# A graph kernel on one core: four accumulator banks for the adjacency products instead of two, and the small products of the edge lots moved into the gate banks

## The chip, the cores and the metric

The kernel runs on one core of one Trainium2 chip. The metric is the device time of one execution in microseconds (us), lower is better. The core has five instruction streams that the profile shows apart: TensorE (PE for its matmuls, PEld for its weight loads, PEq for its sequencer), VectorE (DVE), ScalarE (ACT), GpSimd (POOL) and SyncE (SP, which issues DMAs here). They run side by side and wait for each other through semaphores.

## The reference, cut to what matters

A graph with 6250 nodes of 48 features and 200,000 edges that are sorted by their destination. Five propagation steps with the normalised adjacency, a layer norm, a gated convolution over the edges, and a second layer norm:

```
def _L0_gnn_ref(x, edge_index):
    row = concat(src, loops); col = concat(dst, loops)
    deg = segment_sum(1, col); dinv = rsqrt(deg); w = dinv[row] * dinv[col]
    for _ in range(5):
        h = (1.0 - ALPHA) * segment_sum(w[:, None] * h[row], col) + ALPHA * x
    return h
def _L1_gnn_ref(h, edge_index, edge_attr, distances, atom_z, node_mult, ...):
    gate = _silu(edge_attr @ W1.T + b1) @ W2.T + b2 + adapt_logit
    cw = where(distances < CUTOFF, 0.5 * (cos(pi * distances / CUTOFF) + 1.0), 0.0)
    msg = gate * h[dst] * (cw * mj)[:, None]
    agg = segment_sum(msg, src) / clip(segment_sum(mj, src), 1e-08)
    return layernorm(h + agg) * gamma + beta
x = _layernorm(x + _L0_gnn_ref(x, edge_index))
x = _layernorm(x + _L1_gnn_ref(x, ...))
```

## The kernel before

The kernel builds the adjacency as a dense table of counts, multiplies with it five times, and does the gated convolution after that. Its stages follow each other in time. By the profiled execution: `index_edges` fills the first 160 us or so (it sorts out the edges and writes tables of keys); `adjacency` runs from about 160 to 1448 us; the propagation, which streams the adjacency from memory five times, begins at about 1475 us and goes over into the convolution, which ends at 4288 us.

**The adjacency.** The nodes form `NB` = 49 blocks of 128 (50 with padding). For each block `D` there are 64 groups of 128 edges (`GB` = 64, padded). A *turn* handles `PT` = 8 of these groups, so a block has `NBAT` = 8 turns. In each turn DVE writes two one-hot tiles, `ohb` (128 x 1024, L992) and `ohk` (128 x 784, L994), into one of `OB` = 8 slots; PE multiplies them in `batch` as two groups of four matmuls (L1031), and each group of four fills one accumulator bank of `pA`; ACT copies the bank of each group into the block's row `adj` (L1067, 128 x 392) and, when a block is complete, stores it (L1072, 1568 KB). The group `n` writes bank `n % 2` and first waits, on the semaphore `a_ev`, until ACT has copied group `n - 2` out of that bank. ACT waits on `a_grp` for the group. At the start of each turn PE increments `a_turn`, its *turn mark*.

**The edge lots.** The values of the gates do not depend on the propagation, so they are computed beside other work, in lots of 4096 edges (`NWIN` = 49 lots). 24 lots run inside the adjacency, interleaved with the turns by a list written out in the program; 25 run inside the propagation. The first loop of the adjacency (`DOUBLE` = 1 pass) does four blocks in 32 turns with one lot, the second loop has 23 passes of two blocks in 16 turns with one lot each. A lot has `MC` = 4 chunks of 8 steps (`CT` = 8), and takes this way through the engines:

- DVE's `fields`, `counts` and `ranks` find for each edge the slot in which its row will lie. They need two small products from PE: `labels` (L764, a 128 x 128 product, issued behind turn 0) and `offsets` (L769, 128 x 49, behind turn 4). Both go to the bank `w_pR`. ACT copies the offsets to `w_offb` (L774).
- For each chunk PE transposes the attributes (`transposes`, L731), ACT copies them (L799), PE computes the hidden layer (`hidden`, L740), ACT applies silu (L792, to `w_hid`), and PE computes the gates (`gates`, L749), 8 x 48 = 384 columns of bank `q % 2` of `w_pG`. In the second loop `pe_parts` issues these behind the odd turns: at turn 5 the gates of chunk 0, at 7 those of chunk 1, at 9 chunk 2, at 11 chunk 3.
- DVE's `rows_out` (L894 to L896, in turns 11 to 14) takes the gates into the rows `w_pay`. It waits for the gates and for `w_free`, which POOL gives when its scatter of an earlier chunk has landed.
- POOL scatters the rows to the table of slots: 32 indirect DMAs for each lot (L705), each issued by one instruction. Ahead of step `t` POOL waits for a turn mark of PE (`in_single`), so that the scatters are spread over the turns, two to a turn, a fixed number of turns behind:

```
pool.wait_ge(s_turn, w * MARKS + (DOUBLE * MARKS + 10 + t * MARKS // WT))
```

So the scatter of a lot runs from PE's turn 9 of its own pass to about turn 9 of the next. The order on each engine is the order in which the program is written; nothing reorders it.

## Time and profile before

| what | value |
|---|---|
| time of the kernel before, median of 3 runs | 4324.79 us (4321.98 to 4325.89) |
| time of the profiled execution | 4289.53 us |
| its span, first to last instruction | 4287.8 us |
| mean granted TensorE clock | 0.746 of full speed |
| busy: PE, DVE, POOL, ACT | 2739.1, 2747.3, 2377.7, 1372.9 us |

The time of an execution is what is measured; the span is read from the profile of one execution. That execution is 35.3 us shorter than the median, so durations of the profile are set against 4289.53 and only the difference is carried to the median. No engine is busy for more than 64% of the span, and the stages differ: in the adjacency another thing ends the waits than in the propagation. So the sum of an engine over the span says little here, and the adjacency has to be read by itself. In the rows below, a "releaser" is what ended the idle time of an engine. "issue" is time in which the engine waited for nothing that the profile shows; "remote" is a release that the profile could not put down to an instruction that ended just then.

### The profile page before, as it was taken

What the parts mean: (1) busy time and instruction counts of PE and PEld (TensorE: products, weight loads), DVE (VectorE), ACT (ScalarE), POOL (GpSimd) and SP (SyncE); (2) the same over time, 40 slices, a digit from 0 to 9 for tenths busy, and PEclk for the clock granted to TensorE, in tenths of its full rate; (3) what the DMA queues carried; (4) which work ended last, traced back from release to release, by engine and by line L of the source; (5) the groups of instructions that cost most, each with busy time, mean ns of one, the idle gap of its engine ahead of it and who ended that gap; (6) DMA issues with size and microseconds to landing.
All of it is one profiled execution on the core that took longest, in us unless ns stands there. A gap on an engine that the chain in (4) does not pass through costs nothing. (4 is left out here: it accounts for less than half of the span.)

```text
span 4287.8 us, 105568 instructions
## 1 busy us (share of the span) xinstructions
PE 2739.1 (64%) x35364; PEld 2335.0 (54%) x35364; DVE 2747.3 (64%) x5976; ACT 1372.9 (32%) x4059; POOL 2377.7 (55%) x2008
## 2 busy tenths in 40 slices
PE   0465555555565377787777787777366666666663
PEld 0343344433443366676676676667366666666662
DVE  3877677777776445554455445545787777777777
ACT  0443333333333111111011111111355555555552
POOL 1267777777777355565565555555344444444442
PEclk9955555555555589898998888888688777777776
DMA  4443333333522488787788787786455555555553
GB/s 182 184 157 137 136 137 136 147 141 136 149 89 89 180 287 298 258 309 286 284 296 297 265 295 285 276 284 239 152 203 186 203 187 199 182 203 180 202 183 92
DMA packets 228040, 871.37 MB, mean 203 GB/s; under 512 B 89155, under 2 KB 148419, under 8 KB 182786
## 3 DMA queue, kind: packets, MB, share of 16 engines
q1 hardware_dynamic: 166914, 728.89, 47.8%
q10 hardware_dynamic: 9696, 96.89, 5.7%
q0 software_dynamic: 51232, 42.56, 3.3%
q8 instruction: 171, 2.80, 0.3%
q14 instruction: 27, 0.22, 0.0%
HBM read 670.80 MB, written 197.52 MB: 203 GB/s over the span
## 5 line engine op out<-in xcount | busy, mean ns | idle before, releaser
L705 POOL DMA_INDIRECT slot_table<-w_pay,w_slot x1568 | 1786.5, 1139 | 1117.6 <-PEq L1217 506.6
L1219 PE MATMUL pL<-p_parts,p_adj 128*128 128x144 bf16 x12250 | 976.3, 241 | 360.0 <-issue 254.2
L1219 PEld LDWEIGHTS pL<-p_parts,p_adj 128*128 128x128 bf16 x12250 | 883.4, 105 | 446.2 <-issue 440.7
L1031 PE MATMUL pA<-ohk,ohb 128*128 128x98 bf16 x3200 | 359.7, 274 | 516.7 <-ACT adj L1067 267.6
L1031 PEld LDWEIGHTS pA<-ohk,ohb 128*128 128x128 bf16 x3200 | 256.8, 131 | 649.2 <-ACT adj L1067 339.0
L1587 ACT ACTIVATE h_all<-c_rows,c_ac 128x48 f32<-128x48 f32 x2401 | 561.0, 323 | 70.4 <-DVE c_ac L1558 70.4
L1463 POOL TENSOR_TENSOR c_msg<-c_msg 128x637 f32<-128x637 f32 x196 | 232.7, 1187 | 617.9 <-DVE c_msg L1525 617.9
L1067 ACT ACTIVATE adj<-pA 128x392 bf16<-128x392 f32 x800 | 369.6, 494 | 525.3 <-remote 260.7
L792 ACT ACTIVATE w_hid<-w_pH,b1c 96x512 f32<-96x512 f32 x196 | 133.7, 682 | 909.5 <-PE w_pH L740 444.2
L1662 PE MATMUL cG<-c_tabp,c_ohT 128*128 128x81 bf16 x7056 | 376.2, 224 | 3.2 <-issue 1.6
L1662 PEld LDWEIGHTS cG<-c_tabp,c_ohT 128*128 128x128 bf16 x7056 | 353.2, 114 | 4.5 <-DVE c_msg L1525 2.2
L1270 DVE TENSOR_REDUCE p_acc<-pL 128x144 f32<-128x432 f32 x100 | 53.2, 532 | 446.8 <-PE pL L1219 220.4
L1465 POOL TENSOR_TENSOR c_msg<-c_msg 128x637 f32<-128x637 f32 x196 | 324.6, 1656 | 15.4
L992 DVE TENSOR_TENSOR ohb<-io_k,pair_b 128x1024 bf16<-128x1024 bf16 x400 | 275.2, 688 | 66.9 <-DVE w_pay L896 14.2
L749 PE MATMUL w_pG<-w2T,w_hid 97*128 97x96 f32 x1568 | 292.8, 347 | 7.0 <-issue 7.0
L740 PE MATMUL w_pH<-w_attrT,w1T 80*96 80x512 f32 x392 | 288.8, 829 | 0.0
L1653 PE MATMUL cE<-c_cur,c_ohT 128*128 128x32 bf16 x7203 | 217.6, 181 | 110.1 <-ACT h_all L1603 70.3
L1637 PE MATMUL cO<-c_msg,c_ohs 128*128 128x147 bf16 x2401 | 244.5, 262 | 55.6 <-POOL c_msg L1465 54.3
L1498 DVE TENSOR_SCALAR c_ohT<-c_lanes,c_idx 128x3328 bf16<-128x3328 bf16 x196 | 271.9, 1387 | 6.8 <-DMA c_lanes<-lane_table 6.8
L1653 PEld LDWEIGHTS cE<-c_cur,c_ohT 128*128 128x128 bf16 x7203 | 209.2, 99 | 122.9 <-issue 122.8
L749 PEld LDWEIGHTS w_pG<-w2T,w_hid 97*128 97x128 f32 x1568 | 266.9, 256 | 8.4 <-issue 8.4
L1514 DVE TENSOR_TENSOR c_ohs<-c_iob,c_sl 128x1664 bf16<-128x1664 bf16 x196 | 241.7, 1233 | 0.0
(277 smaller groups left out, 3308.4 us busy)
## 6 DMA issues: line engine op xcount, KB each, us to landing
p_adj<-adj_table SPq DMA_DIRECT2D x250, 1568.0 KB
c_lanes<-lane_table SPq DMA_DIRECT2D x150, 768.0 KB, 6.5
adj_table<-adj ACTq DMA_DIRECT2D x50, 1568.0 KB
c_rows<-slot_table SPq DMA_DIRECT2D x255, 255.0 KB, 4.0
slot_table<-zero SPq DMA_DIRECT2D x42, 1249.5 KB
c_lanes<-lane_table SPq DMA_DIRECT2D x50, 832.0 KB
w_attr<-in_edge_attr_dram SPq DMA_DIRECT2D x49, 640.0 KB
slot_table<-w_pay,w_slot POOLq DMA_INDIRECT x1568
```

Of the source, the lines that this page charges most:

```text
L705: pool.indirect_dma_start(slotT, bass.IndirectOffsetOnAxis(ap=slot[:, t:t + 1], axis=0), pay[:, t, :], None, bounds_check=SLOTS - 1, oob_i ...
L740: nc.tensor.matmul(pH[0:2 * H, 0:n * P], w1T2[:, :], attrT[:, 0:n, :].rearrange("r t e -> r (t e)")).then_inc(s_h, 1)
L749: x_ = nc.tensor.matmul(pG[:, q % 2, i * 2 * H:(i + 1) * 2 * H], hid[:, i, :], w2T2[:, :])
L992: nc.vector.tensor_tensor(ohb[:, b % OB, :, :].rearrange("p q (a t) -> p q a t", t=2), twos(P), pair_b[:, at, :].unsqueeze(2).to_broadcast ...
L1031: m = nc.tensor.matmul(pA[:, n % 2, j * KG:(j + 1) * KG], ohb[:, b % OB, g * (PT // 2) + j, :], ohk[:, b % OB, g * (PT // 2) + j, :])
L1067: nc.scalar.activation(adj[:, u, :, n * PT:(n + 1) * PT].rearrange("p s (j d) -> p s j d", d=GR), pA[:, n % 2, 0:PT // 2 * KG].rearrange(" ...
L1219: x_ = nc.tensor.matmul(pL[:, half, o * H3:(o + 1) * H3], adj[:, q, n * P:(n + 1) * P], parts[:, n, :, :].rearrange("p t f -> p (t f)"), s ...
L1465: nc.gpsimd.tensor_tensor(part(c_, 2), part(c_, 1), upper[:, c_, 1, 0:n, :], ALU.subtract).then_inc(s_r2, 1)
L1498: nc.vector.tensor_scalar(ohT[:, k % 2, 0:2 * n, :].rearrange("p m e -> p (m e)"), lanes[:, c_, 0:2 * n * P], idx[:, :], None, ALU.is_equa ...
L1587: x_ = nc.scalar.activation(gx[:, k % 2, j, 0:H], rows[:, u, CUT[c_] + j, 0:H], ACT.Identity, bias=ac[:, k % 2, j:j + 1])
L1653: m = nc.tensor.matmul(pE[:, j * G:(j + 1) * G], ohT[:, k % 2, j, :], cur[:, u, t, :], start=t == 0, stop=t == 2)
L1662: m = nc.tensor.matmul(g_at(k, j), ohT[:, k % 2, n + j, :], tabp[:, CUT[c_] + j, t, :], start=t == 0, stop=t == 2)
```

## The change

The accumulator `pA` gets four banks in place of two: group `n` writes bank `n % 4` and waits until ACT has copied group `n - 4`. To have the banks, `w_pR` is given up. The labels now go to the free columns 384 to 511 of gate bank 1, the offsets to the columns 384 to 432 of gate bank 0. So that the gates of chunk 0, which write bank 0, do not meet ACT's copy of the offsets, these gates wait in addition for `w_offb` (in the adjacency; not in the propagation, where the order differs). `index_edges`, which runs earlier and had borrowed `w_pR`, gets a bank of its own for that time.

```diff
--- before.py
+++ after.py
@@ -378,7 +378,8 @@
                 pair = ew
                 bad_row = ps("bad_row", [1, 512], c=c)
                 pP = ps("pP", [P, 2, 1024], BF16, c)
-                pC, pZ, pQ = win.pR, win.pG, win.pT
+                pC = ps("pC", [P, 512], c=c)
+                pZ, pQ = win.pG, win.pT
                 s_dst, s_src, s_ew, s_et = s_edges
                 s_io = sem("i_io")
                 s_lo, s_lof, s_cnt, s_pre, s_sum = sem("i_lo"), sem("i_lof"), sem("i_cnt"), sem("i_pre"), sem("i_sum")
@@ -659,7 +660,10 @@
             pT = ps("w_pT", [P, 512], c=c)
             pH = ps("w_pH", [P, 512], c=c)
             pG = ps("w_pG", [P, 2, 512], c=c)
-            pR = ps("w_pR", [P, 512], c=c)
+            GATES = CT // 2 * 2 * H
+            assert GATES + P <= 512 and GATES + NB <= 512
+            offs = pG[:, 0, GATES:GATES + NB]
+            labs = pG[:, 1, GATES:GATES + P]
             seed = dram("seed", [CT * P, 4])
             s_init, s_kf, s_win, s_attr = sem("w_init"), sem("w_kf"), sem("w_win"), sem("w_attr")
             s_T, s_aT, s_h, s_hid, s_g = sem("w_T"), sem("w_aT"), sem("w_h"), sem("w_hid"), sem("w_g")
@@ -740,19 +744,21 @@
                 nc.tensor.matmul(pH[0:2 * H, 0:n * P], w1T2[:, :],
                                  attrT[:, 0:n, :].rearrange("r t e -> r (t e)")).then_inc(s_h, 1)
 
-            def gates(pe, w, q):
+            def gates(pe, w, q, offsets_first):
                 pe.wait_ge(s_hid, w * MC + q + 2)
 
                 pe.wait_ge(s_pay, w * MC + q + 1)
                 pe.sem_inc(s_pe, 1)
+                if q == 0 and offsets_first:
+                    pe.wait_ge(s_offb, w + 1)
                 for i in range(pairs_of(q)):
                     x_ = nc.tensor.matmul(pG[:, q % 2, i * 2 * H:(i + 1) * 2 * H], hid[:, i, :], w2T2[:, :])
                 x_.then_inc(s_g, 1)
 
-            def pe_parts(pe, w, n):
+            def pe_parts(pe, w, n, offsets_first=True):
 
                 if 2 <= n < MC + 2:
-                    gates(pe, w, n - 2)
+                    gates(pe, w, n - 2, offsets_first)
                 if 1 <= n < MC + 1:
                     hidden(pe, w, n - 1)
                 if n < MC:
@@ -761,17 +767,17 @@
             def labels(pe, w):
 
                 pe.wait_ge(s_diag, w + 1)
-                nc.tensor.matmul(pR[:, P:2 * P], ones_w[:, :], diag[:, :]).then_inc(s_lab, 1)
+                nc.tensor.matmul(labs, ones_w[:, :], diag[:, :]).then_inc(s_lab, 1)
 
             def offsets(pe, w):
 
                 pe.wait_ge(s_tot, w + 1)
-                nc.tensor.matmul(pR[:, 0:NB], before[:, :], tot[:, :]).then_inc(s_off, 1)
+                nc.tensor.matmul(offs, before[:, :], tot[:, :]).then_inc(s_off, 1)
 
             def act_offsets(act, w):
 
                 act.wait_ge(s_off, w + 1)
-                nc.scalar.activation(off_b[:, :], pR[:, 0:NB], ACT.Copy).then_inc(s_offb, 1)
+                nc.scalar.activation(off_b[:, :], offs, ACT.Copy).then_inc(s_offb, 1)
 
 
             def act_start(act):
@@ -861,7 +867,7 @@
                 flat = lambda a: a[:, :, :].rearrange("p s j -> p (s j)")
                 step(nc.vector.tensor_tensor_scan(flat(run), flat(cont), flat(oh), 0.0, ALU.mult, ALU.add))
                 dve.wait_ge(s_lab, w + 1)
-                nc.vector.scalar_tensor_tensor(before[:, :], pR[:, P:2 * P], label[:, :], to_here[:, :], ALU.is_equal, ALU.mult)
+                nc.vector.scalar_tensor_tensor(before[:, :], labs, label[:, :], to_here[:, :], ALU.is_equal, ALU.mult)
                 step(nc.vector.tensor_tensor(firsts[:, :], carry[:, :], run[:, :, WT - 1], ALU.subtract))
                 step(nc.vector.scalar_tensor_tensor(tot[:, :], firsts[:, :], last_p[:, :], run[:, :, WT - 1], ALU.mult, ALU.add))
                 dve.sem_inc(s_tot, 1)
@@ -900,7 +906,7 @@
             win.turns, win.chunks = MC + 2, MC
             win.io_s, win.rtop, win.dtop, win.pT = io_s, rtop, dtop, pT
             win.labels, win.act_offsets = labels, act_offsets
-            win.pG, win.pR = pG, pR
+            win.pG = pG
             win.load_keys, win.load_attr = load_keys, load_attr
             win.pool_start, win.scatter, win.pool_end = pool_start, scatter, pool_end
             win.pe_start, win.pe_parts, win.offsets = pe_start, pe_parts, offsets
@@ -919,7 +925,8 @@
                 ohb = sb("ohb", [P, OB, PT, P], BF16, c)
                 ohk = sb("ohk", [P, OB, PT, KG], BF16, c)
                 adj = sb("adj", [P, 2, NB, P], BF16, c)
-                pA = ps("pA", [P, 2, 512], c=c)
+                BANKS = 4
+                pA = ps("pA", [P, BANKS, 512], c=c)
                 s_clear, s_turn, s_poolgo = sem("a_clear"), sem("a_turn"), sem("a_poolgo")
                 s_node = sem("a_node")
                 s_oh, s_grp, s_ev = sem("a_oh"), sem("a_grp"), sem("a_ev")
@@ -1028,7 +1035,7 @@
 
                                 pe.wait_ge(s_ev, D * (2 * NBAT) + n + 1)
                                 for j in range(PT // 2):
-                                    m = nc.tensor.matmul(pA[:, n % 2, j * KG:(j + 1) * KG], ohb[:, b % OB, g * (PT // 2) + j, :],
+                                    m = nc.tensor.matmul(pA[:, n % BANKS, j * KG:(j + 1) * KG], ohb[:, b % OB, g * (PT // 2) + j, :],
                                                          ohk[:, b % OB, g * (PT // 2) + j, :])
                                 m.then_inc(s_grp, 1)
                         with pe.Fori(0, DOUBLE) as w:
@@ -1056,7 +1063,7 @@
 
                         for u in range(2):
                             act.dma_start(adjT[u, :, 0:P], zero[:, 0:P // 2].bitcast(BF16)).then_inc(s_st[u], 16)
-                        act.sem_inc(s_ev, 2)
+                        act.sem_inc(s_ev, BANKS)
 
                         def block_out(D, u, it, parts):
                             for n in range(2 * NBAT):
@@ -1065,10 +1072,10 @@
 
                                     act.wait_ge(s_st[u], it * 16 + 16)
                                 nc.scalar.activation(adj[:, u, :, n * PT:(n + 1) * PT].rearrange("p s (j d) -> p s j d", d=GR),
-                                                     pA[:, n % 2, 0:PT // 2 * KG].rearrange("p (j s d) -> p s j d", s=NB, d=GR), ACT.Copy).then_inc(s_ev, 1)
+                                                     pA[:, n % BANKS, 0:PT // 2 * KG].rearrange("p (j s d) -> p s j d", s=NB, d=GR), ACT.Copy).then_inc(s_ev, 1)
                                 if n % 2:
                                     parts(n // 2)
-                            act.wait_ge(s_ev, D * (2 * NBAT) + 2 * NBAT + 2)
+                            act.wait_ge(s_ev, D * (2 * NBAT) + 2 * NBAT + BANKS)
                             act.dma_start(adjT[bass.ds(D, 1), :, :].rearrange("o p f -> p (o f)"),
                                           adj[:, u, :, :].rearrange("p s d -> p (s d)")).then_inc(s_st[u], 16)
                         with act.Fori(0, DOUBLE) as w:
@@ -1223,7 +1230,7 @@
                                     if piece % 5 == 0 and piece // 5 < TURNS0:
                                         turn = piece // 5 + v * TURNS0
                                         if turn < win.turns:
-                                            win.pe_parts(pe, w, turn)
+                                            win.pe_parts(pe, w, turn, False)
                                     if v == 0 and piece == 3:
                                         win.labels(pe, w)
                                     if v == 0 and piece == 10:
```

No instruction moves to another place. What changes in the order is a wait. This is PE's stream in a pass of the second loop, from the second small product on; `L1031` is the group of four matmuls, `L769` the offsets, `L749` the gates, `i_eT` the name under which the wait for a free bank is printed, and `s_wTc` the one for the one-hots. Before:

```order
L769 MATMUL w_pR<-w_tot,w_before 128x49 [waits w_tot]
L1024 REGISTER_ALU
L1029 REGISTER_ALU [waits s_wTc]
L1031 MATMUL pA<-ohk,ohb 128x98 [waits i_eT]
L1031 MATMUL pA<-ohk,ohb 128x98 x3
L749 MATMUL w_pG<-w2T,w_hid 128x96 [waits w_hid,w_pay]
L749 MATMUL w_pG<-w2T,w_hid 128x96 x3
L736 REGISTER_ALU
```

After the change (line numbers are larger by 4 to 7):

```order
L775 MATMUL w_pG<-w_tot,w_before 128x49 [waits w_tot]
L1031 REGISTER_ALU
L1036 REGISTER_ALU [waits s_wTc]
L1038 MATMUL pA<-ohk,ohb 128x98 [waits i_eT]
L1038 MATMUL pA<-ohk,ohb 128x98 x3
L755 MATMUL w_pG<-w2T,w_hid 128x96 [waits w_hid,w_pay,w_offb]
L755 MATMUL w_pG<-w2T,w_hid 128x96 x3
L740 REGISTER_ALU
```

The rows are the same but for the destination of the offsets and the third wait of the first gates.

## Rows read from the trace of the kernel before

**Rows 1.** Windows by stage: us, busy of each engine, granted clock, DMA share, GB/s

```profile
160.00:258.00 98.00, 63.48 (x420) 43.94 (x421) 84.12 (x185) 47.41 (x98) 38.54 (x33) 0.69 0.45 168
400.00:1400.00 1000.00, 580.24 (x3592) 403.84 (x3591) 702.32 (x1595) 381.32 (x791) 728.73 (x616) 0.54 0.36 131
1400.00:1448.00 48.00, 9.02 (x60) 5.87 (x59) 5.19 (x13) 6.64 (x14) 34.26 (x35) 0.50 0.17 58
1475.00:4288.00 2813.00, 1977.58 (x30559) 1806.63 (x30558) 1761.21 (x3798) 852.88 (x2976) 1440.37 (x1194) 0.83 0.67 237
```

**Rows 2.** Groups by line, 400 to 1400 us: busy, mean ns; idle before, by releaser

```profile
L705 POOL DMA_INDIRECT slot_table<-w_pay,w_slot x616 | 730.1, 1185 | 271.6 <-issue 177.6 <-PEq L1025 93.1 <-DMA slot_table<-w_pay,w_slot 0.9
L1067 ACT ACTIVATE adj<-pA 128x392 bf16<-128x392 f32 x616 | 285.4, 494 | 428.4 <-remote 221.2 <-PE pA L1031 190.7 <-issue 13.7
L1031 PE MATMUL pA<-ohk,ohb 128*128 128x98 bf16 x2464 | 277.3, 274 | 412.8 <-ACT adj L1067 214.6 <-issue 193.1 <-DVE ohk L994 4.2
L749 PE MATMUL w_pG<-w2T,w_hid 97*128 97x96 f32 x624 | 144.8, 408 | 7.0 <-issue 7.0
L894 DVE COPY w_pay<-w_meta 128x24 f32<-128x24 f32 x78 | 14.5, 185 | 214.2 <-remote 128.1 <-PE w_pG L749 53.6 <-POOLq L711 19.8
```

**Rows 3.** Timeline from 804 to 808 us: a scatter beside a long scan

```profile
804.05 3.42 DVE L862 TENSOR_TENSOR_SCAN w_run<-w_cont,w_oh 128x1568 bf16<-128x1568 bf16 x1
804.81 3.44 POOL L705 DMA_INDIRECT slot_table<-w_pay,w_slot  x1 [0.30 <-issue]
```

**Rows 4.** Waits, 400 to 1400 us: us in total, times, longest

```profile
PEld pA L1031 <- ACT adj L1067: 270.8, 210, 9.6
...
POOL slot_table L705 <- PEq L1025: 93.1, 60, 4.2
```

**Rows 5.** Timeline before POOL has run long: start, duration, instruction, idle before

```profile
205.20 0.89 ACT L1067 ACTIVATE adj<-pA 128x392 bf16<-128x392 f32 x2 [0.21 <-PE pA L1031]
```

**Rows 6.** Timeline from 469 to 483 us

```profile
469.92 1.99 PE L749 MATMUL w_pG<-w2T,w_hid 97*128 97x96 f32 x8
...
477.39 0.98 POOL L705 DMA_INDIRECT slot_table<-w_pay,w_slot  x1 [0.30 <-issue]
480.43 0.18 DVE L894 COPY w_pay<-w_meta 128x24 f32<-128x24 f32 x1 [12.70 <-remote]
482.46 1.06 POOL L705 DMA_INDIRECT slot_table<-w_pay,w_slot  x1 [4.09 <-PEq L1025]
```

**Rows 7.** Timeline from 835 to 856 us, another lot

```profile
835.45 0.68 ACT L792 ACTIVATE w_hid<-w_pH,b1c 96x512 f32<-96x512 f32 x1 [3.14 <-remote]
...
837.22 1.25 POOL L705 DMA_INDIRECT slot_table<-w_pay,w_slot  x1 [0.30 <-issue]
838.96 0.50 ACT L1067 ACTIVATE adj<-pA 128x392 bf16<-128x392 f32 x1 [2.82 <-remote]
...
840.56 1.99 PE L749 MATMUL w_pG<-w2T,w_hid 97*128 97x96 f32 x8
...
841.43 0.98 POOL L705 DMA_INDIRECT slot_table<-w_pay,w_slot  x1 [2.96 <-PEq L1025]
...
842.58 0.18 DVE L894 COPY w_pay<-w_meta 128x24 f32<-128x24 f32 x1 [4.96 <-PE w_pG L749]
...
854.18 1.23 POOL L705 DMA_INDIRECT slot_table<-w_pay,w_slot  x1 [2.30 <-PEq L1025]
```

**Rows 8.** Waits in the first loop, 160 to 258 us

```profile
POOL slot_table L705 <- PEq L1025: 85.5, 4, 79.5
```

**Rows 9.** Timeline where the new wait will stand: the offsets' copy and the first gates

```profile
814.28 0.21 ACT L774 ACTIVATE w_offb<-w_pR 128x49 bf16<-128x49 f32 x1 [0.20 <-remote]
...
814.37 1.82 PEld L749 LDWEIGHTS w_pG<-w2T,w_hid 97*128 97x128 f32 x8
```

## Prediction

> **What bounds the kernel now.** I read the profile by windows of its stages first [rows 1], since only the adjacency (160 to 1448 us) is touched. From 400 to 1400 us it is one steady pattern, the second loop. No engine is full there: DVE 702, POOL 729, PE 580 of 1000 us. The reader should see that after 1400 us PE is nearly done (9 us busy in 48) while POOL still scatters 35 times: the stage ends with POOL's last scatter.
>
> The groups by line say why POOL is slow [rows 2]: 616 scatters in 1000 us are 616/32 = 19.25 lots, so one lot takes 1000/19.25 = 51.95 us. Of that, its own instructions are 730.1 us, the gaps between one issue and the next 177.6 us (0.30 us each mostly), together 907.7/19.25 = 47.15 us per lot, about 1.28 us for a bare scatter and more for those that overlap a DVE operation [rows 3]. The rest that a row explains is the wait for PE's turn mark, 93.1 us in 60 waits [rows 4], or 93.1/19.25 = **4.84 us per lot**. So POOL is the pacer, and only these waits can be won.
>
> Why is PE's mark late? PE and its weight loads wait for a bank of `pA`, 270.8 us in 210 waits, the longest 9.6 us [rows 4]. With two banks PE is at most two groups, one turn, ahead of ACT. But ACT's copy takes 0.49 us, and its own waits are not for work: 221.2 us "remote" [rows 2]. The timelines show what this is. Before POOL has run long, ACT follows PE at once [rows 5]. Where POOL has scattered for some 10 us without a break, a result of PE is seen late: the gates of 469.92 us took 1.99 us, but DVE, which had nothing else, took them only at 480.43, 2.06 us after POOL's scatter ended at 478.37 [rows 6]. In another lot ACT's copy stands still until 838.96, 0.49 us after POOL stopped at 838.47 [rows 7]. POOL stops in its turn because the mark is late: it goes on at 841.43, after PE has got its bank. So it is a loop: PE's results are released late while POOL scatters, PE runs out of banks, the mark is late, POOL pauses, the results come through, and all go on. Two such pauses, 2.96 and 2.30 us, make up the 4.84 us of a lot [rows 7].
>
> **The change part by part.**
>
> *Four banks.* PE may run four groups, two turns, ahead of the copies instead of two groups. The work is the same: as many matmuls, as many copies. So each turn mark comes up to one turn earlier relative to the copies, and a turn is worth two scatters, 2 x 1.28 = 2.57 us of POOL. A pause of 2.96 us could shrink by 2.57 us, or, because the releases only come when POOL pauses, it could move by two scatters and stay as long. The trace can't tell these apart; the bounds are 0 and 4.84 us of gain per lot. A second effect is that the gates come sooner. By [rows 7] silu of the last chunk is done at 835.45 + 0.68 = 836.13 us, but PE, in order, is behind a group that waits for its bank until 839.51, and the gates run at 840.56, 4.4 us later than they could. With the groups ahead of them already issued, they are done before POOL pauses, are released with the first pause, and the second one has less cause. I take: the first pause stays (2.96 us), of the second a third (2.30/3 = 0.8 us). A lot is then 47.15 + 2.96 + 0.8 = 50.9 us instead of 51.95. That is -1.1 us for each of the 22 lots whose successor is in the second loop: **-24 us**. The factor of a third is a choice between all and nothing.
>
> *The first loop.* POOL waits for PE 85.5 us, of which 79.5 us are the start (it waits for the first gates, which need 18 turns) and 6.0 us are three others [rows 8]. The start could only move if PE did; before POOL runs, the copies are prompt [rows 5] and PE waits little. I take 2 of the 6.0 us.
>
> *The new wait.* The gates of chunk 0 wait for ACT's copy of the offsets. By [rows 9] that copy starts at 814.28 and takes 0.21 us, and the weight load of the gates starts at 814.37: it would wait until 814.49 or so, 0.1 us, 23 times 0.1 = 2.3 us if nothing covered it. Behind the gates in PE's queue stand a hidden layer, a transposition and the next turn's mark, for which POOL waits. But four banks let the gates arrive sooner, so that they could wait longer; the copy of offsets stands in ACT's order behind the copy of turn 4's groups, and where PE's result is released late (bound: the 9.6 us of [rows 4]), the gates are now late with it. As a cost I take +1 us (the mark is not what POOL waits for in most turns: 60 waits in 616 scatters), the bounds are 0 and 23 x 2 = 46 us.
>
> *Labels and offsets in gate banks.* The two products are as large as before. Reader and writer are ordered by the semaphores of before, except for the one above; The gates of the lot before are read before DVE gets to the labels of the next. 0 us. *The bank of `index_edges`*: 0 us, same work before 160 us. *After 1475 us*: 2813 us [rows 1]; the work there is the same, though the labels and offsets share banks with the gates there too. 0 us, with bounds of -5 and +5.
>
> *Sum.* -24 - 2 + 1 = -25 us: the profiled execution goes from 4289.5 to about 4264.5, and the median, 35.3 us higher, from 4324.8 to **about 4300 us**.
>
> **A rule weighed.** A scatter took 3.44 us beside a scan of 3.42 us [rows 3], where others take 0.98 [rows 6]. The Trainium skill (SBUF — State Buffer, Who interferes with whom) says that only the port pair that DVE and GpSimd share causes contention, as an exclusive lock, and that PE and ACT have ports of their own. With the lock these two agree. But by that rule POOL's scatters would not hold back what ACT and DVE see of PE, and 12.70 us of DVE's wait [rows 6] would have another cause; by the rule the time would be that of rival B, about 4214 us, by the rows 4300 us.
>
> **The rivals.**
>
> *A, the forecast*: one pause goes for the most part, -25 us. For it: two pauses per lot whose second comes when the last gates are late. Chance 0.42.
>
> *B, all of POOL's waits for PE go.* The mechanism: the mark is late only because PE lacks a bank, and with four it does not; POOL never pauses for PE, and the late copies were a matter of depth alone. For it: 270.8 us of PE's waits are for a bank [rows 4]. Against it: where PE's results are released only when POOL pauses, four banks run out as well. Price: 23 x 4.84 = -111 us, about 4214 us. PE, at 580 us busy in 1000, could do it, even with its clock at the low level of 1.2 GHz (0.54 is near it). Chance 0.11.
>
> *C, no change.* The pauses move two scatters later and stay as long, or the new wait eats the gain; or the timed executions have fewer of these late releases than the profiled one. For it: 51.95 us per lot is held by POOL for 91% (47.15), and a pause is needed for each release. Price: between -8 and +8 us, 4317 to 4333. Chance 0.27.
>
> *D, slower.* Place: `rows_out` of the last chunk, at DVE's turn 14. If PE's results come through only in POOL's pause, and the pause comes one turn later (2.57 us), then DVE gets the gates later, POOL's next chunk waits for its rows, and DVE's next `fields` start later. The lot becomes longer by up to 2.57 us: 22 x 2.57 = +57 us, 4381 us. It decides where the pause moves by more than the gates gain: with 4.4 us gained [rows 7] it does not; where the new wait holds the gates of chunk 0 until a pause, it does. Half of its cases would stay under 4345. Chance 0.20.
>
> **How the numbers follow.** What a measurement can tell from no change is about 0.2%, 8.6 us. Faster: A without the few of its cases under 8.6 us (0.38) and B (0.11): 0.49. Same: C and those of A: 0.31. Slower: 0.20. The likeliest is A: 4300 us. The range holds A, C and the half of D: up to 4345; below, A's factor of a third could be zero and the first pause could halve: (4.84 - 1.48) x 22 = 74 us, 4251; some 20 us are added for the first loop's 6.0 us and for the lots with more than two pauses. So 4230 to 4345; it leaves out B (0.11) and half of D (0.10). A's own range is 4270 to 4318.
>
> **What would show it.** In 400 to 1400 us: POOL's waits for PE's mark, now 93.1 us, should be 60 to 75 us (A), under 10 (B), the same (C); a lot 50.9 us (A), 47.2 (B), over 52.5 (D). PE's waits for the bank, 270.8 us, should fall by a third or more in all cases but not vanish, if late release is the cause; if they vanish, the cause was only the depth. The last gates should start within 1 us of silu's end. DVE's idle time ahead of L894 (214.2 us) should fall in A and rise in D. The scatters should keep 1185 ns. The window from the propagation's start to the end should keep 2813 us within 5. The prediction is wrong if the late release is no property of POOL's scatters, or if the pause only moves.

## The result, and the profile after

The changed kernel takes 4363.15 us (median of 4 runs, 4353.74 to 4370.30), the kernel before 4323.39 us beside it: a ratio of 1.0089, 95% interval 1.0058 to 1.0120. It is **slower by 0.9%**, some 40 us. The prediction was 4300 us, within 4230 to 4345. The profiled execution took 4360.42 us, its span is 4358.5 us (before: 4287.8).

All of it lies in the adjacency, as far as the two profiles tell: its last matmul ends at 1487.2 us in place of 1420.0, which is 67 of the 71 us by which the profiled spans differ. (About half of those 71 us is that the profiled execution of before was a short one.) The same windows as in [rows 1] (us, busy of each engine, granted clock, DMA share, GB/s), of the changed kernel:

```profile
400.00:1400.00 1000.00, 489.85 (x3393) 366.03 (x3392) 660.00 (x1502) 341.72 (x747) 688.59 (x579) 0.60 0.35 125
...
1475.00:4288.00 2813.00, 1977.88 (x30529) 1814.76 (x30530) 1732.53 (x3784) 851.66 (x2963) 1466.31 (x1213) 0.83 0.67 239
```

POOL issues 579 scatters in 1000 us in place of 616, and ends its last one of the adjacency at 1512.4 us, where it had ended at 1447.8 before. Groups by line for 400 to 1400 us (POOL's scatter is L709 now, DVE's taking of the gates L900):

```profile
L709 POOL DMA_INDIRECT slot_table<-w_pay,w_slot x579 | 688.8, 1190 | 311.6 <-issue 165.9 <-PEq L1032 144.2 <-SPq L953 1.5
...
L1038 PE MATMUL pA<-ohk,ohb 128*128 128x98 bf16 x2329 | 225.2, 269 | 410.0 <-ACT adj L1074 144.7 <-DVE ohk L1001 140.9 <-issue 124.4
...
L900 DVE COPY w_pay<-w_meta 128x24 f32<-128x24 f32 x72 | 12.8, 178 | 271.3 <-remote 271.3
```

A scatter costs what it did (1190 ns, 1185 before [rows 2]). Three waits changed. PE's for a bank fell, as four banks should make it: 168.1 us in 82 waits for 270.8 in 210 [rows 4]. POOL's for PE's mark rose from 93.1 to 144.2 us. And PE now waits 140.9 us for DVE's one-hots, a wait that was 4.2 us [rows 2]: DVE is what is late next. Per lot the sum is short: 579 scatters are 18.09 lots, so POOL's own work and the gaps between issues are 47.2 us as before, and its waits for the mark are 144.2/18.09 = 8.0 us in place of 4.84. The loss is this wait.

The waits of the same stretch (us in total, times, longest):

```profile
DVE w_pay L900 <- remote: 271.3, 19, 16.2
ACT adj L1074 <- remote: 267.6, 90, 7.3
PEld pA L1038 <- ACT adj L1074: 168.1, 82, 7.5
...
POOL slot_table L709 <- PEq L1032: 144.2, 71, 5.7
...
PE pA L1038 <- DVE ohk L1001: 140.9, 35, 5.7
```

Why can be read off one lot's timeline (start, duration, instruction, idle before and what ended it):

```profile
1021.33 0.98 POOL L709 DMA_INDIRECT slot_table<-w_pay,w_slot  x1 [0.30 <-issue]
...
1021.97 1.99 PE L755 MATMUL w_pG<-w2T,w_hid 97*128 97x96 f32 x8
...
1028.94 0.50 ACT L1074 ACTIVATE adj<-pA 128x392 bf16<-128x392 f32 x1 [3.82 <-remote]
...
1033.19 0.50 ACT L1074 ACTIVATE adj<-pA 128x392 bf16<-128x392 f32 x1 [3.76 <-remote]
...
1036.05 0.98 POOL L709 DMA_INDIRECT slot_table<-w_pay,w_slot  x1 [0.30 <-issue]
1038.94 0.18 DVE L900 COPY w_pay<-w_meta 128x24 f32<-128x24 f32 x1 [16.15 <-remote]
1039.00 2.44 ACT L1074 ACTIVATE adj<-pA 128x392 bf16<-128x392 f32 x6 [5.31 <-remote]
...
1042.15 0.98 POOL L709 DMA_INDIRECT slot_table<-w_pay,w_slot  x1 [5.12 <-PEq L1032]
...
1049.61 0.83 PE L1038 MATMUL pA<-ohk,ohb 128*128 128x98 bf16 x8 [5.65 <-DVE ohk L1001]
...
1050.30 0.98 POOL L709 DMA_INDIRECT slot_table<-w_pay,w_slot  x1 [3.29 <-PEq L1032]
```

POOL starts the lot at 1021.33. The last gates run at 1021.97 and end at 1023.96. DVE takes them at 1038.94, 15 us later and 1.9 us after POOL's twelfth scatter has ended (1037.03) and POOL has stopped to wait for PE's mark. At the same moment ACT gets its groups and copies six. Only then can DVE go on to the next lot's fields and one-hots, so PE waits for DVE until 1049.61 and POOL pauses a second time, 3.29 us. Before the change POOL's first stop was six scatters into the lot [rows 7].

### The profile page after: what moved, and what is told of

It reads as the page before. It is cut to its first block and busy times, and to the rows that moved or that the text cites. A ratio compares the mean times of both kernels' runs of the same rounds, so it can differ in the third digit from the quotient of the medians.

```text
span 4358.5 us, 105568 instructions
## 1 busy us (share of the span) xinstructions
PE 2663.5 (61%) x35364; PEld 2324.4 (53%) x35364; DVE 2744.7 (63%) x5976; ACT 1348.2 (31%) x4059; POOL 2389.6 (55%) x2008
## 5 line engine op out<-in xcount | busy, mean ns | idle before, releaser
L709 POOL DMA_INDIRECT slot_table<-w_pay,w_slot x1568 | 1799.5, 1148 | 1175.8 <-PEq L1224 482.4
L1038 PE MATMUL pA<-ohk,ohb 128*128 128x98 bf16 x3200 | 309.9, 269 | 534.5 <-ACT adj L1074 184.1
L1074 ACT ACTIVATE adj<-pA 128x392 bf16<-128x392 f32 x800 | 350.9, 500 | 612.1 <-remote 344.2
L1644 PE MATMUL cO<-c_msg,c_ohs 128*128 128x147 bf16 x2401 | 244.7, 262 | 55.9 <-POOL c_msg L1472 54.9
L744 PE MATMUL w_pH<-w_attrT,w1T 80*96 80x512 f32 x392 | 270.5, 780 | 1.9 <-issue 1.5
L900 DVE COPY w_pay<-w_meta 128x24 f32<-128x24 f32 x196 | 35.4, 181 | 375.1 <-remote 354.8
```

The costliest lines, as they stand in the source:

```text
L709: pool.indirect_dma_start(slotT, bass.IndirectOffsetOnAxis(ap=slot[:, t:t + 1], axis=0), pay[:, t, :], None, bounds_check=SLOTS - 1, oob_i ...
L744: nc.tensor.matmul(pH[0:2 * H, 0:n * P], w1T2[:, :], attrT[:, 0:n, :].rearrange("r t e -> r (t e)")).then_inc(s_h, 1)
L1038: m = nc.tensor.matmul(pA[:, n % BANKS, j * KG:(j + 1) * KG], ohb[:, b % OB, g * (PT // 2) + j, :], ohk[:, b % OB, g * (PT // 2) + j, :])
L1074: nc.scalar.activation(adj[:, u, :, n * PT:(n + 1) * PT].rearrange("p s (j d) -> p s j d", d=GR), pA[:, n % BANKS, 0:PT // 2 * KG].rearran ...
```

## The experiments

How long this kernel takes depends on when and where it is run by more than the change does: at some times the kernel before takes 3815 to 3821 us, at others 4295 to 4327 us (medians), and one chip (number 14) was found at both. I call them the quick and the slow condition. The result above is of the slow one. Every ratio below is against the kernel before, run beside it on the same chip; times of rows with different numbers of the kernel before are not to be set against each other directly.

The texts on record name four theories. 1: PE's results are handed on late and in their order while POOL scatters, and more banks put more work ahead of the last gates. 2: the moved products and the new wait cost the time. 3: PE's results come through when POOL pauses, and the change moved the pause. 4: PE itself is behind, whatever POOL does.

The times in us and the ratios are medians of all executions (but for the two rows of before without a ratio, which are the profiled execution). The numbers per lot are of the profiled execution alone, worked out from the start and end times of the instructions in its trace, as means over lots 1 to 22 of the second loop: its length (from POOL's first scatter to that of the next lot), the time from the first to the last `rows_out` (r0 to r3), when the last gates end after r0, and how long they were late (r3 less the later of the gates' end and POOL's release of the rows, which its sequencer gives once it has passed the eight scatters of the lot's first chunk; it runs up to three scatters ahead of the engine). "First pause" is the step of the lot ahead of which POOL first stands for over 0.5 us, in most lots.

```
kernel, call                      us      ratio (interval)         lot    first pause   gates end  r3     late
before, profile shown             4289.5  -                        52.1   step 6        16.1       17.6   1.6
changed, profile shown            4363.2  1.0089 (1.0058-1.0120)   54.8   step 10-12     8.1       20.9  10.7
e6 before, slow                   4323.8  -                        53.0   step 6        17.2       17.9   0.7
e5 changed, slow                  4356.9  1.0067 (1.0040-1.0094)   54.9   step 10-12     7.9       21.2  11.2
e7 changed, depth 2, slow         4325.6  1.0005 (0.9988-1.0022)   53.1   step 6        17.0       18.3   1.3
e8 changed, depth 3, slow         4316.6  0.9987 (0.9969-1.0005)   52.4   step 6-10     13.0       17.4   4.1
e9 gates ahead, slow              4343.2  1.0042 (1.0022-1.0062)   53.5   step 4        15.1       17.0   0.9
e10 marks later, slow             4361.2  1.0093 (1.0064-1.0122)   54.6   step 8-10      8.4       21.0   8.7
e18 changed + pause, slow         4261.9  0.9929 (0.9902-0.9957)   50.8   step 4         7.7       14.3   0.1
e1 changed, depth 2, quick        3818.7  1.0004 (0.9996-1.0013)   48.5   none           8.4       14.6   0.1
e11 changed + pause, quick        3819.7  1.0001 (0.9990-1.0011)   48.8   none           7.5       14.9   0.1
```

**Depth without banks (e1, e2, e7, e8).** The changed kernel, but PE is held to the copy of the group two (or three) before:

```diff
-                        act.sem_inc(s_ev, BANKS)
+                        act.sem_inc(s_ev, 2)
...
-                            act.wait_ge(s_ev, D * (2 * NBAT) + 2 * NBAT + BANKS)
+                            act.wait_ge(s_ev, D * (2 * NBAT) + 2 * NBAT + 2)
```

The first two of these runs met the quick condition:

> The changed kernel with four banks, but PE waits until the group two before has been copied out, as before the change; the moved labels and offsets and the new wait for the offsets stay. Theory 1 (order in the queue): while POOL scatters without a break, PE's finished work is handed on late and in its order, about 1 us per matmul; with four banks two more groups stand ahead of the last gates, rows_out of the last chunk comes later, and POOL's pause with it. Then this kernel is like the one before: 4324 us within 9, a lot of 52 us, POOL's first pause near step 6. Theory 2 (the moves): the cost comes from the new wait or from sharing the gate banks. Then it stays near 4363 us, a lot of 54.8 us.

> The same with PE waiting for the copy of the group three before. Theory 1: between the two, 4330 to 4360 us, a lot of 52.5 to 54.5 us, POOL's first pause near steps 8 to 10. Theory 2: near 4363 us.

Depth two gave 1.0004, and a depth of three (e2) 1.0010 (1.0002 to 1.0019). This did not tell the theories apart, since the traces show no late result there. A window of e1's propagation, then its waits for 400 to 1400 us:

```profile
1400.00:2400.00 1000.00, 901.20 (x12034) 840.75 (x12032) 686.23 (x2003) 162.94 (x241) 772.90 (x695) 0.97 0.98 384
```

```profile
DVE w_pay L900 <- POOLq L715: 163.9, 38, 8.6
...
POOL slot_table L709 <- PEq L1032: 10.7, 35, 0.3
```

POOL scatters without one wait over 0.3 us for PE, and DVE waits for POOL's release alone. The propagation is the larger part of the difference between the conditions: 12034 matmuls in 1000 us at 384 GB/s, against 8912 and 286 GB/s in the kernel before in the slow condition (1500 to 2500 us). The adjacency's last matmul ends at 1321.4 us, about 100 us sooner than in the profile shown of before.

Then again, in the slow condition:

> Four banks, but PE waits for the copy of the group two before; the moved products and the new wait stay. On a chip where the kernel before takes some 4325 us. Theory 1 (order in the queue of late results): like before, 4325 within 9 us, a lot of 52 us, first pause near step 6 to 8. Theory 2 (the moves, the new wait): near 4360 us.

> The same with the copy of the group three before. Theory 1: 4330 to 4360 us, a lot of 52.5 to 54.5 us, the first pause near steps 8 to 10. Theory 2: near 4360 us.

Depth two gives 1.0005 (0.9988 to 1.0022): **the moved products and the new wait cost nothing that can be measured (7 us)**, and the loss is due to the depth. Theory 2 falls. Depth three was expected at 4330 to 4360 us and takes 4316.57, no different from before (0.9987, the interval holds 1). Its row in the table goes with that: the gates end 4 us sooner than in e6, and are taken half a microsecond sooner. The first pause moves with the depth: step 6 at two, 6 to 10 at three, 10 to 12 at four.

**The change once more (e5), and the kernel before (e6).**

> The changed kernel as it is, since the first four runs were on a chip where the kernel before takes 3819 us and PE's results are handed on at once (no copy over 1 us late in 736), so that neither theory had anything to act on there. Theory 1 (order in the queue of late results): on a chip of that kind the change does nothing, a ratio of 1.000 within 0.002; on a chip where the kernel before takes some 4320 us it is slower by 0.6 to 1.2%, with POOL's pauses at steps 10 to 12 and 16. Theory 2 (the moves, the new wait): slower on either chip, by 0.5% or more.

> The kernel before, for its profile on the chip of this call. Theory 1: at 3819 us no waits of POOL for PE's mark of more than 0.5 us, and copies at once behind PE's groups with two banks as well; at 4320 us two pauses of 2 to 3 us per lot. Theory 2 says nothing of it.

In the slow condition 1.0067, so the loss repeats. The profile of before taken beside it (e6) has lots of 53.0 us, not 52.1, and POOL waits more for PE than the 93.1 us of [rows 4]:

```profile
POOL slot_table L705 <- PEq L1025: 111.8, 45, 4.6
```

The execution whose rows stand ahead of the prediction was a short one, 35 us below the median; 54.9 less 53.0 us, by 22 lots, is 41 us, and the two executions differ by 38 us.

**Gates ahead (e4, e9), and marks later (e3, e10).** In e9 PE issues the lot's work of an odd turn ahead of that turn's groups; in e10 POOL's steps each wait for one mark more:

```diff
-                                batch(2 * w + 2 * DOUBLE + turn // NBAT, turn % NBAT)
                                 if turn % 2 and turn // 2 < win.turns:
                                     win.pe_parts(pe, w, turn // 2)
+                                batch(2 * w + 2 * DOUBLE + turn // NBAT, turn % NBAT)
```

```diff
-                                pool.wait_ge(s_turn, w * MARKS + (DOUBLE * MARKS + 10 + t * MARKS // WT))
+                                pool.wait_ge(s_turn, w * MARKS + (DOUBLE * MARKS + 11 + t * MARKS // WT))
```

> The changed kernel, with the lot's work of an odd turn issued ahead of that turn's two groups. Theory 1: two groups fewer stand ahead of the last gates, DVE takes them 4 us or more earlier, a lot takes 50.5 to 53 us, in all 4280 to 4325 us. Theory 2: 4360 us within 9.

> The changed kernel with POOL waiting for one turn mark more ahead of each step. Theory 1: the pause comes two scatters earlier in its count, at 8 to 10, the last gates are taken earlier, a lot takes 52 to 53.5 us, in all 4320 to 4345 us. Theory 2: 4360 us or more.

e9 gave 1.0042, between the kernel before and the changed one, where I had expected the whole loss back (4280 to 4325 us; measured 4343.22). Its r3 came 3.9 us sooner than in the changed kernel. Whether it took back a part of the loss is not sure: its interval (1.0022 to 1.0062) overlaps that of e5. e10 took back nothing, 1.0093, and there my expectation (4320 to 4345 us) was wrong. The pause did come two scatters earlier in its count, but POOL had started the lot 2.4 us later for the same reason, and it stopped for the very same mark of PE (step 10 then waits for the mark that step 12 waited for), with r3 at 21.0 us as in the changed kernel. What matters is at which mark of PE POOL stops. The same two kernels had been run in the quick condition:

> The changed kernel, but in the second loop POOL's step t waits for one turn mark more (11 + t/2 in place of 10 + t/2), which gives back the lead that the two extra banks gave. Theory 1: POOL's first long pause comes two scatters earlier in its count (at 8 to 10 in place of 10 to 12), the last gates are taken earlier, and a lot takes 52 to 53.5 us, in all 4320 to 4345 us. Theory 2: the wait for the mark only gets longer, 4363 us or more.

> The changed kernel, but in the second loop PE issues the lot's work of an odd turn (gates, hidden layer, transposes) ahead of that turn's two groups and not behind them. Theory 1: the last gates have two groups fewer ahead of them in the queue (some 8 us at 1 us per matmul), DVE takes them earlier by 4 us or more, and a lot takes 50.5 to 53 us, in all 4280 to 4325 us. Theory 2: no change from 4363 us beyond 9 us.

Both were like the kernel before there: 1.0004 (0.9995 to 1.0013) and 1.0003 (0.9994 to 1.0012).

**A pause on purpose (e11, e12, e14 to e18).** If PE's results come through when POOL stands, then a short stop at the right place should win back the loss. Ahead of step 4 of each lot POOL waits for the last gates, that is for the semaphore on which DVE's `rows_out` waits (the line that hands `s_g` over is left out here):

```diff
                                 pool.wait_ge(s_turn, w * MARKS + (DOUBLE * MARKS + 10 + t * MARKS // WT))
+                                if t == 4:
+                                    pool.wait_ge(win.s_g, w * win.chunks + win.chunks + 1)
```

> The changed kernel, and in the second loop POOL waits ahead of step 4 until the lot's last gates are done (the semaphore that DVE's rows_out waits for). Where the kernel before takes some 4325 us: theory 3 (PE's results come through only when POOL pauses, and the change moved the first pause from step 6 to step 10 or 12): the last rows_out comes 13 us or less behind the first one in place of 21, the pause costs 2 to 3 us, and a lot takes 49.5 to 51.5 us in place of 54.9, in all 4240 to 4295 us. Rival theory 4 (PE itself is behind, since its own work of the lot is slow whatever POOL does): POOL waits at step 4 for as long as the gates took before, 8 us or more, and a lot stays at 54 us or longer, 4345 us or more. On a chip of the 3819 us kind both say no change within 10 us.

The same with two banks, and with a depth of three:

> The same wait of POOL ahead of step 4 in the kernel before. Theory 3: the pause that came at step 6 comes at step 4 and on purpose; the last gates start later than with four banks (2 to 4 us behind silu), so POOL waits 3 to 5 us, and a lot takes 51 to 53 us: 4300 to 4335 us, above the same with four banks by 20 us or more. Theory 4: 4345 us or more.

> The changed kernel with a depth of three and the pause ahead of step 4. Theory 3: within 10 us of the same with a depth of four, 4240 to 4305 us. Theory 4: 4330 us or more.

And the first kernel again:

> The changed kernel with POOL waiting ahead of step 4 until the lot's last gates are done. Where the kernel before takes some 4325 us: theory 3 (PE's results come through only when POOL pauses): the last rows_out comes 13 us or less behind the first one in place of 21, a lot takes 49.5 to 51.5 us in place of 54.9, in all 4240 to 4295 us. Theory 4 (PE itself is behind, whatever POOL does): POOL waits at step 4 for 8 us or more and a lot stays at 54 us or longer, 4345 us or more. On a chip of the 3820 us kind nothing changes.

> The changed kernel with POOL waiting ahead of step 4 until the lot's last gates are done. Where the kernel before takes some 4325 us: theory 3 (PE's results come through only when POOL pauses): the last rows_out comes 13 to 15 us behind the first one in place of 21, a lot takes 49.5 to 51.5 us in place of 54.9, in all 4240 to 4295 us. Theory 4 (PE itself is behind, whatever POOL does): POOL waits at step 4 for 8 us or more and a lot stays at 54 us or longer, 4345 us or more. Where it takes some 3820 us nothing changes.

> The changed kernel with POOL waiting ahead of step 4 until the lot's last gates are done. Where the kernel before takes some 4325 us: theory 3 (PE's results come through only when POOL pauses): the last rows_out comes 13 to 15 us behind the first one in place of 21, a lot takes 49.5 to 51.5 us in place of 54.9, in all 4240 to 4295 us. Theory 4 (PE itself is behind, whatever POOL does): POOL waits at step 4 for 8 us or more and a lot stays at 54 us or longer, 4345 us or more. Where it takes some 3820 us nothing changes.

> The changed kernel with POOL waiting ahead of step 4 until the lot's last gates are done, once more. Where the kernel before takes some 4325 us: theory 3: the last rows_out 13 to 15 us behind the first one in place of 21, a lot of 49.5 to 51.5 us, in all 4240 to 4295 us. Theory 4: POOL waits at step 4 for 8 us or more and a lot stays at 54 us or longer, 4345 us or more. Where it takes some 3820 us nothing changes.

In the quick condition it changes nothing beyond 0.1% (e11 1.0001, e15 1.0010, e16 1.0004 without one execution of 10343 us, e17 1.0002; with two banks, e12, 1.0000; with a depth of three, e14, 1.0006). In the slow condition (e18) it takes **4261.89 us against 4294.80, ratio 0.9929, 0.9902 to 0.9957**: faster than the kernel before by 0.7%, within what theory 3 said and outside theory 4. (The changed kernel without the pause was not run beside it.) Its waits for 400 to 1400 us, and the timeline at one pause:

```profile
DVE w_pay L900 <- POOLq L715: 156.6, 20, 8.9
...
POOL slot_table L709 <- remote: 36.2, 18, 2.3
POOL slot_table L709 <- PEq L1035: 14.3, 33, 2.2
```

```profile
971.99 1.99 PE L755 MATMUL w_pG<-w2T,w_hid 97*128 97x96 f32 x8
...
976.54 0.98 POOL L709 DMA_INDIRECT slot_table<-w_pay,w_slot  x1 [0.30 <-issue]
...
978.92 2.44 ACT L1077 ACTIVATE adj<-pA 128x392 bf16<-128x392 f32 x6 [1.04 <-PE pA L1041]
...
979.71 0.98 POOL L709 DMA_INDIRECT slot_table<-w_pay,w_slot  x1 [2.19 <-remote]
...
981.66 0.32 DVE L900 COPY w_pay<-w_meta 128x24 f32<-128x24 f32 x1 [8.84 <-POOLq L715]
```

The last gates ended at 973.98; POOL stops at 977.52, within 1.4 us ACT gets its groups, and after 2.19 us POOL goes on. Instead of 8 us or more of waiting (theory 4) it is 1.8 to 2.3 us in 20 of 23 lots, and POOL's 144.2 us of waits for PE become 14.3 + 36.2 us. DVE now waits for POOL's release and not for the gates. A lot takes 50.8 us. How much of this the pause would give with two banks in the slow condition was not measured.

**Is the work late, or only the word of it?** The traces also hold the times at which each semaphore was raised. In e1 the last gates of a lot raise theirs 14 ns after their end in the trace, in every one of lots 1 to 22. In the changed kernel (shown profile) it is 12.8 us on the mean, up to 15.8; in the lot above the gates end at 1023.96 and the semaphore rises at 1038.92. Then four groups raise theirs 59 ns apart, up to 1039.16. Groups of PE never start less than 180 ns apart in any trace, so four of them cannot have been computed in those 0.24 us: they were done, and their signals were held back. In the second loop of the changed kernel 89 neighbouring group signals are less than 100 ns apart; in the profiles of the quick condition (e1 to e4, e11 to e17) none are less than 179.

**One scatter of eight (e13).** POOL issues the first scatter of each chunk only, in all lots, so most rows are not written:

> The changed kernel with one scatter in eight (the first of each chunk) and without the other seven, in all lots; those rows are not written, so this leaves out most of the scatter. Theory 3: no copy of a PE group is late by more than 1 us anywhere in the adjacency (121 to 127 of 736 are with all scatters), and a lot takes 36 to 44 us. Theory 4: copies are late as before, a lot stays above 50 us.

It met the quick condition: 3607.5 us (two executions), ratio 0.9446, and PE's passes are 40.8 us apart. This shows that POOL's scatter holds a lot at 48.5 us there and the other engines could do 41, but as to late results it says nothing, since there are none in that condition anyway.

## Why the prediction was wrong

**What bounds the stage: right.** POOL's scatter with its waits for PE is the pace; a scatter is unchanged at 1190 ns, and behind the adjacency's last matmul the profiled kernels differ by 3.5 us.

**The loop of late results: right, and it carried the other way.** While POOL scatters without a break PE's signals come through some 4.3 us apart, and the rest when POOL pauses: e18 shows it by the pause it makes.

**The step that failed** is, in *Four banks*: "With the groups ahead of them already issued, they are done before POOL pauses, are released with the first pause, and the second one has less cause. I take: the first pause stays". The gates did come sooner, and by 8.0 us (16.1 to 8.1 us after r0), not by 4.4. But the first pause did not stay at step 6. PE could give POOL its marks for two to three turns more before it ran out of banks, so POOL ran on to step 10 or 12, and with it moved the moment at which the gates' signal comes through: r3 came 3.2 us later than before. (Why the two banks are worth two to three turns and not one, no run separates.) The gates were ready sooner, but nobody was told. In the terms of the sum: the first pause was put at 2.96 us and the second at 0.8; on the mean of lots 1 to 22 POOL stands 4.9 us in steps 0 to 13 and 3.2 us behind them (2.9 and 2.1 us in the profile of before), and the stage's waits are 8.0 us per lot against the 3.8 forecast.

**The rival that came true** is D, at 4381 us and a chance of 0.20; measured 4363. Its place (`rows_out` of the last chunk) and its sign were right. Its deciding point was not: I set a shift of the pause of 2.57 us against the 4.4 us that the gates gain. The shift was 4 to 6 scatters, 5 to 8 us, and the gates' gain hardly counts against it, since what ends DVE's wait is the pause and not the gates. Its price per lot, up to 2.57 us, was near: 54.9 less 53.0 is 1.9 us, or 2.7 us against the profile shown. The second pause, at step 16, follows from it: DVE is late with the one-hots (140.9 us of PE's waits for 4.2). D's sign was there as well: DVE's idle time ahead of `rows_out` rose from 214.2 to 271.3 us.

**The reading behind it.** I put the 12.70 us that DVE waited in [rows 6] down to the gates alone. `rows_out` of the last chunk also waits for POOL's release of the lot's first chunk. In the profile of before this came at 15.5 us after r0 and the gates ended at 16.1, so `rows_out` was only 1.6 us late on the mean (0.7 in e6). Two banks kept the two nearly together, so there was little to win. Besides, the two pauses of [rows 7] add up to 5.26 us, not to the 4.84 of the mean lot that they were said to make up.

**The other terms.** The new wait and the moves: +1 us with a bound of 46; measured nothing (e7, 1.0005 within 0.0017, 7 us). The first loop: POOL's first scatter at 203.75 us for 203.61 and that of lot 2 at 308.8 for 308.3, so the 2 us of gain did not come. **Rival B** (no late results, POOL at its floor): it is what the quick condition shows (e1: 10.7 us of POOL waits, none over 0.3), but there two banks do as well. The Trainium skill (SBUF — State Buffer, Who interferes with whom) says of the ports of SBUF that PE and ACT never wait on anyone. The traces in the quick condition agree (0 of 736 copies over 1 us late in e1). In the slow one some 130 of 736 are late in the changed kernel and some 165 in the kernel before; what is late there is PE's signal, which a rule on ports does not cover, so concluding rival B from it was a step too far.

**Left open:** what holds PE's signals back in the slow condition. In the changed kernel's trace they come 4.3 us apart, for four matmuls each, while POOL scatters (1024.62, 1028.94, 1033.19), and in their order; as shown above, at least the groups that come through together had been computed. In the same condition the propagation has 8912 matmuls where the other has 12034. Whether this has the same cause, no run tells.

## What to carry to other kernels

A deeper buffer moves the place at which a chain of engines comes to rest. Where one engine's results reach others late until another engine rests, ask where that rest will fall, and not only how much sooner the result is ready. If such a rest is needed, put it where the result is ready: about 2 us of waiting at step 4 turned a loss of 0.7 to 0.9% into a gain of 0.7% here (30 to 40 us slower than the kernel before, and 33 us faster, some 3 us per lot between them, from different chips), and cost nothing measurable where it was not needed. How much of it two banks with the pause would give in the slow condition is not known.

Read a wait for two things by both: compute for each when it was given. And where the work's end and the time at which its semaphore rose are both in the trace, compare them, since they can lie 15 us apart.

## What the runs showed of the hardware that was not expected

The same program, the kernel before, has two levels of time, and all its executions at one time and place were at one of them: 3819 us beside e1 and 4327 us beside e5, the slower 13% longer, at nearly the same granted clock (mostly 0.75 to 0.77 of full speed in the first, 0.74 to 0.77 in the second). In the slower one PE's signals lag by up to 15.8 us while POOL issues indirect DMAs, though the matmuls are done, and the adjacency stream of the propagation runs at 284 GB/s (e6) against 384 (e1). The four banks cost 0.7 to 0.9% in one and, by e3, e4 and e11, which keep them, nothing in the other (the changed kernel as it is was not run there); the pause on purpose was worth 0.7% in one and nothing in the other.
